# An adaLN-Mamba-MoE layer on one core: z projected into the experts' banks at other slots, norms and three GpSimd products moved, and the kept residual added by TensorE

## What is computed

```python
h = layernorm(x) * (1 + ca) + sa                  # z1 in the kernel after the modulation
xn = layernorm(h) * norm_g + norm_b
for d in (forward, backward):                     # E = 256 inner channels, N = 16 states
    u, z = split(xn @ Win[d].T)
    u = silu(causal_conv4(u) + convb)
    dtr, B, C = split(u @ Wx[d].T);  dt = softplus(dtr @ Wdt[d].T + bdt)
    state[t] = exp(dt * A) * state[t-1] + (dt * u) * B[t]
    y = (sum_n state * C + u * D) * silu(z)
    out[d] = y @ Wout[d].T
x2 = x + ga * (h + out[0] + out[1])
h2 = layernorm(x2) * (1 + cb) + sb
out_x = x2 + gb * (sum of the top 2 of 8 experts' swiglu(h2), weighted, + shared swiglu(h2))
```

## Time and profile before

| | us |
|---|---|
| median of 3 runs | 2459.84 (2459.71 to 2462.65) |
| profiled execution: its time / its span | 2461.73 / 2459.9 |
| busy: VectorE | 2236.6 (91% of the span) |
| busy: TensorE | 2066.5 (84%) |
| busy: GpSimd | 2023.6 (82%) |
| busy: ScalarE | 1511.4 (61%) |

### The profile page before, as it was taken

One profiled execution on the slowest core, in us unless ns is written; L12 is line 12 of the kernel. 1 busy time (PEld: TensorE's weight loads), 2 busy tenths in 40 slices (PEclk: granted clock), 3 DMA queues, 4 the chain that ended last, 5 costly groups with the idle time before them and its releaser, 6 DMA issues. The chain is left out here.

```text
span 2459.9 us, 31865 instructions
## 1 busy us (share of the span) xinstructions
PE 2066.5 (84%) x9957; PEld 1312.1 (53%) x9957; DVE 2236.6 (91%) x3546; ACT 1511.4 (61%) x2483; POOL 2023.6 (82%) x1334
## 2 busy tenths in 40 slices
PE   6678988889888887978888898887978888898868
PEld 2445655545555554655555565554655555465545
DVE  4999999999999999999999999999999999999962
ACT  4656666576656666666676656666666576666633
POOL 2777979889798897979889797897979889797855
PEclk7678989989899999999999898999999999999989
DMA  5333343333444334333433334333433343333310
GB/s 149 131 136 122 134 135 132 136 122 126 135 133 135 122 126 134 135 134 129 140 123 125 134 130 143 126 121 126 140 134 127 133 129 125 129 135 136 123 67 27
DMA packets 124061, 312.42 MB, mean 127 GB/s; under 512 B 19700, under 2 KB 46308, under 8 KB 123892
## 3 DMA queue, kind: packets, MB, share of 16 engines
q1 hardware_dynamic: 123892, 310.39, 37.2%
HBM read 303.74 MB, written 6.60 MB: 126 GB/s over the span
## 5 line engine op out<-in xcount | busy, mean ns | idle before, releaser
L490 POOL TENSOR_TENSOR bt<-v,bb 128x1024 f32<-128x1024 f32 x511 | 1207.0, 2363 | 181.9 <-DVE psA L923 167.2
L923 DVE TENSOR_TENSOR_SCAN psA<-psA,bt 128x512 f32<-128x512 f32 x1024 | 1196.6, 1214 | 56.7 <-POOL bt L490 37.3
L675 ACT ACTIVATE psA<-dt,aneg 128x512 f32<-128x512 f32 x1024 | 689.3, 688 | 723.3 <-DVE g L933 723.1
L1181 PEld LDWEIGHTS psY<-ident,g 128*128 128x128 f32 x4096 | 509.4, 151 | 461.2 <-DVE g L933 256.0
L1181 PE MATMUL psY<-ident,g 128*128 128x128 f32 x4096 | 604.4, 292 | 166.4 <-DVE g L933 165.2
L933 DVE TENSOR_TENSOR g<-psA,cb 128x512 f32<-128x512 f32 x1024 | 672.6, 676 | 0.0
L580 POOL TENSOR_TENSOR act<-pf,gf 128x512 f32<-128x512 f32 x288 | 367.0, 1274 | 163.4 <-DVE pf L1022 151.0
L1281 PE MATMUL F<-h2T,w 128*128 128x512 f32 x576 | 325.5, 648 | 126.0 <-DVE pf L1022 125.9
L1329 PE MATMUL F<-w,act 128*128 128x128 f32 x2304 | 308.3, 277 | 13.6 <-POOL act L580 13.1
L1329 PEld LDWEIGHTS F<-w,act 128*128 128x128 f32 x2304 | 280.7, 192 | 31.1 <-POOL act L580 26.6
L1197 PE MATMUL psP<-xnT,wcT 128*128 128x512 f32 x496 | 258.2, 647 | 9.6 <-DVE zs L1085 9.2
(11 more groups left out here) (185 smaller groups left out, 1936.4 us busy)
## 6 DMA issues: line engine op xcount, KB each, us to landing
bb<-bc_rows SPq DMA_DIRECT2D x256, 512.0 KB, 3.7
cb<-bc_rows SPq DMA_DIRECT2D x256, 512.0 KB, 3.6
wB<-w_rows SPq DMA_DIRECT2D x80, 256.0 KB, 3.9
x<-in_L_attn_x SPq DMA_DIRECT2D x16, 256.0 KB, 4.3
out_x<-osb SPq DMA_DIRECT2D x16, 256.0 KB, 4.5
modA<-mod_table SPq DMA_DIRECT2D x15, 192.0 KB, 4.4
w<-in_L_ffn_ew SPq DMA_DIRECT2D x2, 1024.0 KB, 7.6
bc_rows<-xd SPq DMA_DIRECT2D x32, 64.0 KB, 3.1
```

Of the source, the lines that this page charges most:

```text
L490: g.tensor_tensor(bt[:, n % 2, :, :], v[d][:, :, :], bb[:, n // 2 % 2, n % 2, :].unsqueeze(1).broadcast_to([P, NH, T]), ALU.mult).then_inc ...
L675: s.activation(psA[:, half * T:half * T + T], dt_[d][:, half, :], ACT.Exp, scale=aneg[d][:, half, n:n + 1]).then_inc(a_s, 1)
L923: w.tensor_tensor_scan(ah, ah, bt[:, n % 2, half, :][:, order], 0.0, ALU.mult, ALU.add)\
L1181: last = m.matmul(psY[:, half * T + i * P:half * T + i * P + P], g_[:, n % 2, half, i * P:i * P + P], ident[:, :], is_transpose=True, star ...
```

## The change

- Half 0 of z goes to bank `F0` and half 1 to `F1`, which the experts do not use then, and no longer through `psP`. For the forward direction TensorE and ScalarE do them at slots 29 and 30, VectorE at 30 and 31; for the backward direction TensorE and ScalarE at slots 2 and 5, VectorE both at slot 6. `ln1p` stays where it was.
- The norms move forward: x's statistics from slot 8 to 3, 1/std 9 to 4, normalising 10 to 6, modulation 12 to 7, second statistics 13 to 8, its 1/std 14 to 9, second normalising 15 to 10, transpose 16 to 12.
- On GpSimd the first product of `hx` moves from slot 21 to 23, the second from 23 to 31, `wg` from 25 to 6, and the backward `v` from 11 to 12.
- `x2`: TensorE adds `hxK` by four more matmuls with `ident` at the end of each projection group; ScalarE copies `F2` to `x2` at slot 4, ahead of that slot's exponentials; VectorE's addition is gone.

```diff
-U_AT, XD_AT, DT_AT, LN1P_AT, Z_AT, V_AT = 0, 6, 7, 9, 9, 11
-STAT_SLOT, RSTD_SLOT, Z1_SLOT, H1_SLOT, STAT2_SLOT, RSTD2_SLOT, XNORM_SLOT, XN_SLOT = 8, 9, 10, 12, 13, 14, 15, 16
-HX_SLOT, WG_SLOT = 21, 25
+U_AT, XD_AT, DT_AT, LN1P_AT = 0, 6, 7, 9
+V_SLOT = (30, 12)
+Z_SLOTS, ZS_SLOTS = ((29, 30), (2, 5)), ((30, 31), (6, 6))
+STAT_SLOT, RSTD_SLOT, Z1_SLOT, H1_SLOT, STAT2_SLOT, RSTD2_SLOT, XNORM_SLOT, XN_SLOT = 3, 4, 6, 7, 8, 9, 10, 12
+HX_SLOTS, WG_SLOT = (23, 31), 6
...
+            def turn_z(b, d, slot):
+
+                if slot in Z_SLOTS[d]:
+                    half = Z_SLOTS[d].index(slot)
+                    act_e.wait_ge(z_full, 4 * b + 2 * d + half + 1)
+                    s.activation(th[:, 2 + half, :], (F0, F1)[half][:, :], ACT.Tanh).then_inc(zt_s, 1)
...
-                if k - Z_AT in (0, 2):
-                    silu(b, d, Z, (k - Z_AT) // 2)
...
+            def keep_x2(fb):
+
+                act_e.wait_ge(F2_full, (DOWN + NE) * fb + PROJ + 1)
+                wait(act_e, o_s, 2 * fb)
+                s.activation(x2[:, :, :], F2[:, :], ACT.Copy).then_inc(F2_free, 1)
...
+                    if ffn and slot == X2_SLOT:
+                        keep_x2(b - 1)
                     if ffn:
                         expert_turns(b - 1, up_at(slot - 1))
...
+            def finish_z(b, d, slot):
+                for half in range(NH):
+                    if slot == ZS_SLOTS[d][half]:
+                        dve.wait_ge(zt_s, 4 * b + 2 * d + half + 1)
+                        w.scalar_tensor_tensor(zs[d][:, half, :], th[:, 2 + half, :], 1.0, (F0, F1)[half][:, :],
+                                               ALU.add, ALU.mult).then_inc(z_free, 1)
...
-                if slot == X2_SLOT:
-                    dve.wait_ge(F2_full, (DOWN + NE) * fb + PROJ + 1)
-                    dve.wait_ge(hxK_s, fb + 1)
-                    wait(dve, o_s, 2 * fb)
-                    w.tensor_tensor(x2[:, :, :], F2[:, :].rearrange("p (k c) -> p k c", c=D), hxK[:, :, :], ALU.add)\
-                        .then_inc(F2_free, 1)
...
+            def project_z(b, d, slot):
+
+                if slot in Z_SLOTS[d]:
+                    half = Z_SLOTS[d].index(slot)
+                    if d == 0:
+                        wait(pe, (pf_s, F1_free)[half], 2 * NE * (b - 1))
+                    else:
+                        pe.wait_ge(z_free, 4 * b + half + 1)
+                    m.matmul((F0, F1)[half][:, :], wzT[d][:, half, :], xnT[:, PAD:PAD + T], start=True, stop=True)\
+                        .then_inc(z_full, 1)
...
+                        pe.wait_ge(z_free, min(4 * fb + 8, 4 * NB))
...
                         for k in range(2 * NH):
-                            last = m.matmul(F2[:, i * D:i * D + D], yg[k // NH][:, k % NH, i * P:i * P + P],
-                                            wg[:, k // NH, k % NH, :], start=(k == 0), stop=(k == 2 * NH - 1))
+                            m.matmul(F2[:, i * D:i * D + D], yg[k // NH][:, k % NH, i * P:i * P + P],
+                                     wg[:, k // NH, k % NH, :], start=(k == 0), stop=False)
+                        last = m.matmul(F2[:, i * D:i * D + D], ident[:, :], hxK[:, i, :], start=False, stop=True)
```

More of the change, by code:

```diff
@@ L250, in adaln_mamba_moe @@
         th_s = sem("th_s")
+        z_full = sem("z_full")
+        z_free = sem("z_free")
+        zt_s = sem("zt_s")
         sp_s = sem("sp_s")
@@ L605, in side @@
                         make_dt(prep_f, 0)
-                    if slot == PREP_SLOT[0] + V_AT:
+                    if slot == V_SLOT[0]:
                         make_v(prep_f, 0)
@@ L609, in side @@
                     make_dt(b, 1)
-                if prep_b and slot == PREP_SLOT[1] + V_AT:
+                if prep_b and slot == V_SLOT[1]:
                     make_v(b, 1)
@@ L686, in take, with silu @@
                 act_e.wait_ge(pP_full, PIECES * b + pos + 1)
[L688 to L696, removed]
+            def silu(b, d, half):
+                take(b, piece(d, U, half))
+                s.activation(psP[:, :], psP[:, :], ACT.Identity, scale=0.5,
+                             bias=convb[d][:, half:half + 1]).then_inc(xh_s, 1)
+                act_e.wait_ge(xh_s, 4 * b + 2 * d + half + 1)
+                s.activation(th[:, half, :], psP[:, :], ACT.Tanh).then_inc(th_s, 1)
+            def turn_z(b, d, slot):
[3 more added lines that the diff above has]
+                    s.activation(th[:, 2 + half, :], (F0, F1)[half][:, :], ACT.Tanh).then_inc(zt_s, 1)
             def prep(b, d, k):
                 if k - U_AT in (1, 4):
-                    silu(b, d, U, (k - U_AT) // 3)
+                    silu(b, d, (k - U_AT) // 3)
                 if k == XD_AT:
@@ L747, in side @@
                     prep(prep_f, 0, slot - PREP_SLOT[0])
+                    turn_z(prep_f, 0, slot)
                 if prep_b:
                     prep(b, 1, slot - PREP_SLOT[1])
+                    turn_z(b, 1, slot)
             def expert_turns(fb, k):
@@ L801, in first_z @@
             def first_z(bank, half):
-                act_e.wait_ge(pP_full, piece(0, Z, half) + 1)
-                s.activation(th[:, 2 + half, :], bank, ACT.Tanh).then_inc(th_s, 1)
+                act_e.wait_ge(z_full, half + 1)
+                s.activation(th[:, 2 + half, :], bank, ACT.Tanh).then_inc(zt_s, 1)
             norms(0, Z1_SLOT)
@@ L831, in _ @@
             exps(0, 0, 0, 0)
-            first_z(F2[:, :], 0)
-            first_z(psP[:, :], 1)
+            first_z(F0[:, :], 0)
+            first_z(F1[:, :], 1)
             act_e.wait_ge(const_ok, CONSTS)
@@ L1210, in prep @@
                     m.matmul(psP[:, :], wdtT[d][:, k - DT_AT, :], xd[0:R, :], start=True, stop=True).then_inc(pP_full, 1)
-                if k - Z_AT in (0, 2):
-                    half = (k - Z_AT) // 2
-                    open_piece(Z, half)
-                    m.matmul(psP[:, :], wzT[d][:, half, :], xnT[:, PAD:PAD + T], start=True, stop=True)\
-                        .then_inc(pP_full, 1)
+            def project_z(b, d, slot):
[7 more added lines that the diff above has]
+                        .then_inc(z_full, 1)
             def skip_and_turn(bank, d, half):
@@ L1258, in ffn_side @@
                     last.then_inc(turned, 1)
-                if slot == XN_SLOT:
+                if slot == POST_F_SLOT:
                     pe.wait_ge(wtsT_s, fb + 1)
@@ L1357, in _ @@
             m.matmul(psY[:, 0:T], wdtT[0][:, 1, :], xd[0:R, :], start=True, stop=True).then_inc(pP_full, 1)
-            m.matmul(F2[:, :], wzT[0][:, 0, :], xnT[:, PAD:PAD + T], start=True, stop=True).then_inc(pP_full, 1)
-            m.matmul(psP[:, :], wzT[0][:, 1, :], xnT[:, PAD:PAD + T], start=True, stop=True).then_inc(pP_full, 1)
+            m.matmul(F0[:, :], wzT[0][:, 0, :], xnT[:, PAD:PAD + T], start=True, stop=True).then_inc(z_full, 1)
+            m.matmul(F1[:, :], wzT[0][:, 1, :], xnT[:, PAD:PAD + T], start=True, stop=True).then_inc(z_full, 1)
             pe.wait_ge(diag_ok, 2 * NH)
```

41 lines of the change are left out of this document (23 added, 18 removed).

## The result

The changed kernel takes 2437.39 us (median of 4 runs, 2435.85 to 2438.78), the kernel before beside it 2459.78 (2459.39 to 2462.65): ratio 0.9906, 95% interval 0.9889 to 0.9923. It is faster by 22.4 us; the forecast was 32.0 us faster, that is 2427.8 in a range of 2414 to 2442. One execution of the kernel before (2939) and one of x2_back (3554), both from experiments 1 to 4, ran in a slower state, and the ratios leave them out.

What follows compares the result with a forecast made beforehand. VectorE, 91% busy, was taken to bound the kernel. Terms summed to -2.26 a body, -31.7 over 14 bodies, together about -0.3 at the ends: -32.0 from 2459.8 gives 2427.8, range 2414 to 2442.

Steps and rivals of the forecast that it cites:

- Slots 12 and 13: Backward zs leaves slot 12, -0.6; second statistics leave slot 13, -1.58 if bt of slot 14 comes in time.
- So it just fits, with 0.1 to spare: GpSimd's full queue through slots 8 to 14: bt of slot 14 ends at 36.2, VectorE wants it at 36.3.
- a rival (1 us late, 14 more): GpSimd or ScalarE takes part back: bt of slot 14 1 us late, 14 more, 2442; chance 0.13.
- Slots 3 and 6: VectorE gets x's statistics at slot 3 and both backward zs at slot 6, +0.9 each.
- Slot 4: VectorE's addition goes, -0.7, but a wait of 0.15 for ScalarE's copy stays: -0.55, bounds -0.7 and +0.3.
- Slot 10 and slots 29 to 31: z's tanh wait is really ln1p's; exponentials start earlier: -0.5 at slot 10, +0.1 at 29 to 31.
- Slots 21 to 28: Without hx ahead, bt of slot 24 comes 0.93 earlier and the TensorE-ScalarE chain moves with it: -0.93, bounds -0.5 and -1.7.
- waits of pf for tf: Sign of being wrong: VectorE's pf waiting for tf more than 1.2 a body.
- Slot 8: x's statistics exchanged for the second ones; wg waits for modG with nobody delayed: 0.
- the rival of slots 3 and 4: Slower: at TensorE's half clock there, the late copy holds slot 5's exponentials; +4.8 a body, 2527; chance 0.05.
- The tail: Body 16: the projection stands on the path alone, 8 more pieces, +0.95; the copy takes the addition's place evenly.
- The start and body 0: z no longer holds psP, so the first u's 0.96 goes: -0.9; body 0 about 0.

Runs made afterwards that it cites:

- x2_back: The changed kernel with the x2 part (ScalarE's copy and the four matmuls) undone; 2436.48 us, ratio 0.9899.
- experiments 1 to 4: The kernel before with x2 alone (2467.82 us), the changed kernel without x2 (2436.48), the kernel before with z alone (2481.48), with hx and wg alone (2452.12).
- warm_mid: The changed kernel with unread matmuls, ten calls a body, in TensorE's idle places of the full bodies; 2428.53 us, ratio 0.9847.
- v14: The changed kernel with GpSimd's backward v at slot 14 instead of 12; 2435.53 us, ratio 0.9905.
- before_warm: The kernel before with eleven unread matmul calls added in its tail, at the same slots as warm_tail; 2458.02 us, ratio 0.9982.
- warm_tail: The changed kernel with eleven unread matmul calls added at the end of body 15 and in body 16; 2430.13 us, ratio 0.9884.
- stat2_10: The changed kernel with the second statistics at slot 10, their 1/std and normalising at 11; 2447.98 us, ratio 0.9958.
- stat2_10_v14: The changed kernel with the second statistics at slot 10, 1/std and normalising at 11, and backward v at slot 14; 2437.16 us, ratio 0.9904.
- z_alone: The kernel before with only z's part (banks F0 and F1, z's slots); 2481.48 us, ratio 1.0072.
- hx_alone: The kernel before with only the hx products at slots 23 and 31 and wg at slot 6; 2452.12 us, ratio 0.9946.
- experiments 8 and 12: Eleven unread matmul calls added in the tail of the changed kernel (2430.13 us) and of the kernel before (2458.02 us).
- warm_mid_s2v14: The unread matmuls of warm_mid added in the full bodies of stat2_10_v14; 2420.44 us, ratio 0.9811.

## Why the prediction was right, and where it was off

The direction, the mechanism and the range held; the size was 9.6 us too large. Between the spans the measured sum is 9.0 off: 5.6 in the bodies and 4.7 in the tail, less 1.4 by luck in the start. By the prediction's steps:

- **Slots 12 and 13** (-0.6 and -1.58): measured -0.59 and about -1.3. "So it just fits, with 0.1 to spare" is the step that failed by 0.3: bt of slot 14 is waited for in every full body, by 0.27 in the one shown (act 1251.27, bt 1252.49 to 1254.86). The prediction had named a bt wait at slot 14 as a sign of being wrong, and as a rival (1 us late, 14 more); it came at a quarter of that size. With the clock raised in warm_mid it is gone, and without v in the queue (v14) too; neither brings the 0.3 back whole.
- **Slots 3 and 6** (+0.9 each): +0.88 each.
- **Slot 4** (-0.55): -0.63 in some bodies, -0.33 in others, when y's sum and projection come later after low clock; mean -0.5. In these others VectorE waits 0.31 to 0.42 for the copy, where the prediction wanted less than 0.3; in warm_mid no body has this wait.
- **Slot 10 and slots 29 to 31** (-0.5 and +0.1): -0.52 and +0.11. The removed waits for z's tanh came back as 1.7 for the exponentials, as said.
- **Slots 21 to 28** (-0.93): -0.92. bt of slot 24 is still late by 0.91, where 0.6 was forecast, and waits of pf for tf are 1.24 a body, just above the 1.2 that was named as a sign of being wrong: 0.6 of them are the new wait at slot 27, which the -0.93 has in it.
- **Slot 8** (0): 0. wg waited 3.5 for modG with nobody behind it.
- **Slot 9**, no term in the sum: +0.24 in every other body, an expert's tanh late by TensorE's low clock in slots 7 and 8. The prediction saw that slots that lose z matmuls could see the low level more, and weighed it only as the rival of slots 3 and 4; it gave it no price.
- Sum -2.26, measured -1.87, 5.6 us less over 14 bodies. By slots, 0.29 of the missing 0.39 stand in slot 13, 0.11 in slot 9 and 0.08 in slot 4, and small differences elsewhere give 0.09 back. warm_mid, where the clock is 0.98 in place of 0.94, has ten bodies of fourteen at 144.6 to 144.8, the 144.7 that the prediction named, and 144.82 on the mean: 3.8 of the 5.6 us come back.
- **The tail** (+0.95): +5.7, the term most wrong. 0.9 is the projection. Of the other 4.8, 2.1 are the same work at a lower clock ahead of the projection (at full clock 11.0 in both before_warm and warm_tail); the rest lies with the experts, where TensorE's 16 products at 2382.29 took 3.33 for 2.05. It is not a fixed cost of the change: v14 and stat2_10 have this very tail's code and take 87.8 and 88.0, which is the forecast +0.95 and a little; stat2_10_v14 takes 92.3. Where a stretch of low clock falls decides 5 us. But the x2 part has a share in it. Of the seven kernels that have it and no added matmuls in the tail, five take 54.7 from the 16 products to the end; the four without it (before, x2_back, z_alone, hx_alone) all take 53.1 there, also the two whose first stage took 15.3.
- **The start and body 0** (-0.9): -2.3, but this is no measure of the change. before and before_warm have the same code there and take 178.9 and 174.6.
- The Trainium skill (TensorE: Matmul & The Clock Gate, Part 1) says that the clock falls to half rate after idling. The prediction drew from it that slots 9 to 12 could see the low level more; there the clock is 0.97 to 1.00 (before 0.88 to 1.00), and the rows show the low level in slots 7 and 8 and in the tail. The trace agrees with the rule in kind: in the tail the 8 pieces of y's sum ahead of the idle time of 2.78 us took 1.25 and those behind it 1.97, and the clock is 1.00 in the first stage of experiments 8 and 12, where added matmuls stand in the idle times. But it does not tell the two tails apart, whose idle times are the same.

What stays open: why the clock comes back ahead of the projection in some kernels and not in others, after equal idle times; why the low level falls on the experts' first pairs in before_warm and a step later in warm_tail, with the same matmuls added and first stages of equal length; what holds slot 9 in warm_mid_s2v14; and what the norms would be worth without z. No run separated these.

## What to carry to other kernels

A wait that the trace names is worth its time only if the next supplier is early: here z's 3.2 us a body came back as 3.0 of exponentials, and z moved alone made the kernel slower, because GpSimd's bt for slots 13 and 14 did not come sooner. Price a set of moves as a set, with the queue that feeds the next scan followed through, and take a slack of 0.1 as none. And when an edit takes matmuls out of gaps or makes gaps longer, give TensorE's granted clock a term: take the time at both levels for what follows the gap, and give it a range also where the edit leaves the gaps alone, as in this tail. Try matmuls that nobody reads in idle places; they were worth 7 us in one tail, 4 in the bodies (14 beside GpSimd's moves), and nothing in another tail.

## What the runs showed that was not expected

- In the changed tail TensorE idles 2.78, 1.18 and 0.78 us between pieces, and its mean clock over these 15.3 us is 0.55; in the kernel before it idles the same times and has 0.74 over 13.2 us; with added matmuls between the same pieces it is 1.00.
- Added work makes the kernel faster: 300 more matmuls in the trace (10385 for 10085, by 150 calls) raised TensorE's busy time from 2079.6 to 2133.1 and came with 3.8 us less over the full bodies.
- The same tail code took 87.8 to 92.8 us in different kernels (86.9 to 89.0 without the x2 part), and the same start 174.6 to 178.9. An experiment that differs by less than this in its ends says nothing about its edit. The mean period of the bodies repeated within 0.05 in the three pairs of kernels with the same bodies (146.96 and 146.95 for before and before_warm).
